# A graph attention layer with residual norm: f2 spread by one transpose, f1 made early, bounds moved among the table work, two tiles requested ahead

## The reference

```
in_fts = W @ x.T
f1 = (w1 @ in_fts).T + b1            # one number for each row
f2 = (w2 @ in_fts).T + b2            # one number for each column
logits = leaky_relu(f1 + f2.T)       # slope 0.01
coefs = softmax(logits + where(adj > 0, 0, -1e9), axis=-1)
out = layernorm(x + coefs @ x)       # over the 128 columns, eps 1e-5
```

## Time and profile before

| | us |
|---|---|
| median of 3 runs | 318.31 |
| lowest, highest | 314.53, 329.12 |
| the profiled execution | 315.71 |
| its span, first to last instruction | 313.9 |
| TensorE, matmuls busy | 266.3 |
| VectorE busy | 243.3 |
| ScalarE busy | 189.2 |
| GpSimd busy | 49.0 |

### The profile page before, as it was taken

The page is one execution under the profiler, slowest core; times in us unless marked ns, Lnnn a source line. Parts: engine busy times, 40 slices in busy tenths (PEclk is TensorE's granted clock), DMA queues, the critical chain, the costliest instruction groups (busy, mean ns, idle before and its releaser), DMA issues.

```text
span 313.9 us, 5895 instructions
## 1 busy us (share of the span) xinstructions
PE 266.3 (85%) x2178; PEld 225.0 (72%) x2178; DVE 243.3 (78%) x338; ACT 189.2 (60%) x270; POOL 49.0 (16%) x50
## 2 busy tenths in 40 slices
PE   1889580394999959996999999999999999999980
PEld 1745480273788848884888888888888888888860
DVE  1768794739575859996998999999699779899432
ACT  0619377619989195739857974987877792131130
POOL 3000013000000000350072027008101200331200
PEclk9999895599699999997999999999999999999997
DMA  4999949409999999999999999999999999510011
GB/s 128 309 326 244 204 106 216 82 2 226 309 310 305 303 304 301 304 304 275 303 310 289 325 333 325 291 319 320 290 291 318 322 276 269 139 36 1 0 45 25
DMA packets 25598, 73.64 MB, mean 235 GB/s; under 512 B 3440, under 2 KB 7664, under 8 KB 25584
## 3 DMA queue, kind: packets, MB, share of 16 engines
q1 hardware_dynamic: 14800, 36.77, 41.4%
q10 hardware_dynamic: 10144, 34.61, 38.1%
q0 software_dynamic: 640, 2.10, 3.2%
HBM read 71.37 MB, written 2.10 MB: 234 GB/s over the span
## 4 chain that ended last, share of the span: by engine, by line
PE 54%; ACT 12%; DVE 11%; DMA 10%; issue 6%; ACTq 3%; POOL 3%; POOLq 0%; DVEq 0%
PE ps L960 51%; ACT sgn L405 8%; DMA nat<-in_adj 7%; DMA msk<-in_x 2%; ACTq L271 2%; DVE msk L623 1%; POOL nmr L366 1%; PE ps L940 1%; ACT post L498 1%; DVE f2raw L557 1%; DVE sgn L553 1%; DVE bt L600 1%; ACT bt L437 1%; DVE mn L615 1%; DVE post L594 1%
## 5 line engine op out<-in xcount | busy, mean ns | idle before, releaser
L960 PE MATMUL ps<-bt,msk 128*128 128x258 f16 x2048 | 237.5, 278 | 14.3 <-ACT post L498 10.6
L960 PEld LDWEIGHTS ps<-bt,msk 128*128 128x128 fp8e5 x2048 | 203.3, 100 | 48.1 <-issue 11.4
L405 ACT ACTIVATE sgn<-ps,nf1l 128x1024 int8<-128x1024 f32 x128 | 132.1, 1137 | 19.8 <-DVE mn L615 11.1
L610 DVE TENSOR_SCALAR mn<-nat 128x4096 int8<-128x4096 int32 x32 | 72.6, 2283 | 27.2 <-DMA nat<-in_adj 26.3
L498 ACT ACTIVATE post<-ps,ac 128x258 f32<-128x258 f32 x64 | 27.8, 502 | 44.7 <-PE ps L960 44.7
L366 POOL TENSOR_SCALAR nmr<-mv 128x4 f32<-128x4 f32 x7 | 21.2, 3025 | 199.8 <-DVE mv L775 199.8
L623 DVE STREAM_TRANSPOSE msk<-mn 128x1024 uint32<-128x1024 uint32 x32 | 37.9, 1220 | 0.0
L615 DVE SCALAR_TENSOR_TENSOR mn<-sgn,mn 128x1024 uint32<-128x1024 uint32 x32 | 37.7, 1217 | 0.0
L505 ACT ACTIVATE ybt<-ybt,nmr,rstd 128x128 f32<-128x128 f32 x28 | 11.5, 484 | 17.0 <-POOL nmr L371 17.0
L628 DVE TENSOR_SCALAR msk<-msk 128x1024 uint32<-128x1024 uint32 x32 | 20.1, 666 | 0.0
L600 DVE SCALAR_TENSOR_TENSOR bt<-bt,post 128x1024 f16<-128x1024 f16 x8 | 9.8, 1219 | 6.7 <-ACT bt L437 6.7
(11 more groups left out here) (93 smaller groups left out, 109.4 us busy)
## 6 DMA issues: line engine op xcount, KB each, us to landing
nat<-in_adj SPq DMA_DIRECT2D x64, 512.0 KB, 18.9
nat<-in_adj ACTq DMA_DIRECT2D x64, 512.0 KB, 15.4
xn<-in_x POOLq DMA_DIRECT2D x4, 512.0 KB, 8.6
out<-ybt SPq DMA_DIRECT2D x28, 64.0 KB, 21.0
msk<-in_x SPq DMA_DIRECT2D x8, 128.0 KB, 6.0
msk<-in_x ACTq DMA_DIRECT2D x8, 128.0 KB, 7.0
out<-post SPq DMA_DIRECT2D x16, 16.0 KB, 1.5
wsb<-in_L_gnn_W SPq DMA_DIRECT2D x1, 64.0 KB, 2.3
```

What stands on the lines that cost most here:

```text
L405: ins = act.activation(sgn[:, c, g * JA:(g + 1) * JA], f2b, ACT.Sign, bias=nf1l[:, bass.ds(G * t + g, 1)], scale=-1.0)
L610: dve.tensor_scalar(mn[:, c % 2], nat[:, c], 0, EDGE, ALU.is_gt, ALU.mult).then_inc(cast_done, 1)
L960: ins = pe.matmul(ps[:, 2 * s + m, 0:2 * DV], mask_f[c][m][:, n // KB, n % KB, :], btv[m][:, n, :], start=(n == 0), stop=(n == NK - 1))
```

## The change

1. `f2b` is a tile in SBUF, written by one VectorE transpose of 32x32 blocks (`f2_rows`), whose input repeats each value of `f2l` 32 times. `spread_f2`, the four matmuls behind it and their PSUM banks go.
2. w1 and w2 are loaded as two rows (`wrow`), and TensorE turns them into `w12`. The first chunk of x is requested ahead of W, w1 and w2.
3. All of `turn_x`, `xT_out` and `f1_columns` run before the first edge sums, in two PSUM banks by turns; statistics go to bank 3. `signs` can take another piece of work between its second and third activation.
4. VectorE's list is ordered anew: `spread_f1(1)`, f1n, the statistics, the bounds, `ea` and `flag` stand between the steps of the tables, and the flag is no longer behind them all. TensorE sums xsum ahead of tile 0's m = 0 chunks; the fourth set of signs stands before the flag.
5. Tiles 4 and 5 are requested by both queues before the flag, each once the cast of tile 0 or 1 has freed its slot.

The diff, without declarations of semaphores and the general branch:

```diff
+        f2b = sb("f2b", [P, JA], F32)
+        wrow = sb("wrow", [2, P], F32)
...
-        f2b = ps[:, 4:6, :].rearrange("p b n -> p (b n)")
         FIRST = 3
-        turn_bank = [0, 1, 2, 0, 2, 3, 2, 3]
...
+            for a in range(A // 2):
+                load_x(sp, a, 0)
             sp.dma_start(wsb[:, :], W).then_inc(w_in, 16)
-            for h in range(BCH):
+            for h in range(1, BCH):
...
+            for c in range(EARLY):
+                load_tile(1, c)
             go = fast(sp)
...
+                load_quad(1, first=EARLY)
...
-            act.dma_start(w12[:, 0:1], w1.rearrange("o h -> h o")).then_inc(w12_in, 16)
-            act.dma_start(w12[:, 1:2], w2.rearrange("o h -> h o")).then_inc(w12_in, 16)
-            for h in range(BCH):
+            for a in range(A // 2, A):
+                load_x(act, a, 0)
+            act.dma_start(wrow[0:1, :], w1).then_inc(w12_in, 16)
+            act.dma_start(wrow[1:2, :], w2).then_inc(w12_in, 16)
+            for h in range(1, BCH):
...
-            def signs(t, c):
...
+                    ins = act.activation(sgn[:, c, g * JA:(g + 1) * JA], f2b[:, :], ACT.Sign,
                                          bias=nf1l[:, bass.ds(G * t + g, 1)], scale=-1.0)
+                    if g == 1 and between:
+                        between()
...
-                act.activation(xT[:, b * 512:(b + 1) * 512], ps[:, turn_bank[b], :], ACT.Copy).then_inc(xT_ready, 1)
+                act.activation(xT[:, b * 512:(b + 1) * 512], ps[:, 4 + b % 2, :], ACT.Copy).then_inc(xT_ready, 1)
...
             xT_out(1)
             f2_sums(4, 8)
             xT_out(2)
+            square(0)
+            xT_out(3)
             load_far(1, 1)
-            xT_out(3)
             act.wait_ge(f2l_ready, 1)
             act.activation(de[:, :], f2l[:, :], ACT.Exp, scale=NEG_SLOPE).then_inc(exp_ready, 1)
             scales(1, de)
+            xT_out(4)
             act.wait_ge(nF2_ready, 1)
             act.activation(be[:, :], f2l[:, :], ACT.Exp, bias=nF2[:, 0:1]).then_inc(exp_ready, 1)
             scales(0, be)
-            act.wait_ge(f2b_made, 1)
+            xT_out(5)
+            act.wait_ge(f2b_ready, 1)
             act.wait_ge(nf1l_ready, 1)
-            signs(0, 0)
+            signs(0, 0, between=lambda: xT_out(6))
             split_x(1, 0)
-            square(0)
+            xT_out(7)
             split_x(1, 1)
+            square(1)
+            square(2)
+            split_x(1, 2)
+            square(3)
             load_far(2, 2)
-            square(1)
-            xT_out(4)
-            split_x(1, 2)
-            xT_out(5)
             split_x(1, 3)
-            xT_out(6)
+            signs(1, 1, between=lambda: split_x(0, 0))
+            split_x(0, 1)
             load_far(3, 3)
-            split_x(0, 0)
-            xT_out(7)
-            square(2)
-            square(3)
-            signs(1, 1)
-            split_x(0, 1)
             split_x(0, 2)
-            split_x(0, 3)
-            signs(2, 2)
+            act.wait_ge(cast_done, 1)
+            load_far(QT, 0)
+            signs(2, 2, between=lambda: split_x(0, 3))
+            act.wait_ge(cast_done, 2)
+            load_far(QT + 1, 1)
+            act.wait_ge(nf1l_ready, 2)
+            signs(3, 3)
             act.wait_ge(ea_ready, 1)
             act.activation(ac[:, :, :], ea[:, :, :], ACT.Exp).then_inc(rows_ready, 1)
             act.wait_ge(rows_ready, 1)
...
-                ahead(0, 0, 4)
+                ahead(0, 0, 4, True)
                 evacuate(0, 0, 0)
-                ahead(0, 1, 4)
+                ahead(0, 1, 4, True)
                 evacuate(0, 0, 1)
...
-            def spread_f2(half):
-
-                n = NK // 2
-                dve.tensor_tensor(spread[:, half * 512:(half + 1) * 512].rearrange("p (b r k) -> p b r k", r=SQ, k=KB),
-                                  f2l[:, half * n:(half + 1) * n].rearrange("p (b o k) -> p b o k", o=1, k=KB
-                                                                            ).to_broadcast([P, NB // 2, SQ, KB]),
-                                  pick[:, None, :, None].to_broadcast([P, NB // 2, SQ, KB]),
-                                  ALU.mult).then_inc(spread_ready, 1)
+            def f2_rows():
+
+                dve.transpose(f2b.rearrange("p (b r k) -> p b k r", r=SQ, k=KB),
+                              f2l.rearrange("p (b k o) -> p b k o", k=KB, o=1).to_broadcast([P, NB, KB, SQ])
+                              ).then_inc(f2b_ready, 1)
...
+            dve.wait_ge(w12_made, 1)
+            dve.tensor_copy(w12[:, :], ps[:, 6, 256:258]).then_inc(w12_ready, 1)
             dve.wait_ge(v_made, 1)
...
-            spread_f2(0)
-            spread_f2(1)
+            f2_rows()
             stat_max(0, 0, 2)
...
             scale_x(1, 0)
-            scale_x(1, 1)
             cast(0, 0, 0)
             low_den(1)
+            scale_x(1, 1)
+            combine(0, 0)
             low_x(1, 0)
+            turn(0, 0)
             scale_x(1, 2)
-            combine(0, 0)
+            plus(0, 0)
             low_x(1, 1)
-            turn(0, 0)
-            dve.wait_ge(f2b_made, 1)
+            spread_f1(1, FIRST * KB, NK, 7, 0)
             scale_x(1, 3)
-            plus(0, 0)
             low_x(1, 2)
+            dve.wait_ge(nf1_made, 2)
+            for g in range(G):
+                rows = slice(g * SQ, (g + 1) * SQ)
+                dve.tensor_scalar(f1n[rows, :], ps[rows, 6, 128:256].rearrange("p (t g) -> p t g", g=G)[:, :, g], -1.0,
+                                  None, ALU.mult).then_inc(f1n_ready, 1)
+            dve.tensor_copy(nf1l[:, FIRST * KB:], ps[:, 6, 128 + FIRST * KB:256]).then_inc(nf1l_ready, 1)
             dve.wait_ge(cs_ready[0], 1)
             scale_x(0, 0)
             low_x(1, 3)
+            dve.wait_ge(f1n_ready, G)
+            dve.tensor_reduce(stat[:, 2:3], f1n[:, :], AX_X, ALU.max, apply_absolute_value=True)
+            dve.wait_ge(squares_ready, BCH)
+            dve.tensor_reduce(stat[:, 3:4], squares[:, :], AX_X, ALU.add).then_inc(stat_ready, 1)
             low_den(0)
             scale_x(0, 1)
+            stat_max(1, 2, 4)
             cast(1, 1, 0)
             low_x(0, 0)
+            stat_out(1, 2, 4)
             scale_x(0, 2)
-            low_x(0, 1)
-            combine(1, 1)
-            scale_x(0, 3)
-            turn(1, 1)
-            low_x(0, 2)
-            plus(1, 1)
-            low_x(0, 3)
-            spread_f1(1, FIRST * KB, NK, 7, 384)
-            dve.wait_ge(squares_ready, BCH)
-            dve.tensor_reduce(stat[:, 3:4], squares[:, :], AX_X, ALU.add)
-            dve.wait_ge(nf1_made, 2)
-            for g in range(G):
-                rows = slice(g * SQ, (g + 1) * SQ)
-                dve.tensor_scalar(f1n[rows, :], ps[rows, 7, 128:256].rearrange("p (t g) -> p t g", g=G)[:, :, g], -1.0,
-                                  None, ALU.mult).then_inc(f1n_ready, 1)
-            dve.tensor_copy(nf1l[:, FIRST * KB:], ps[:, 7, 128 + FIRST * KB:256]).then_inc(nf1l_ready, 1)
-            dve.wait_ge(f1n_ready, G)
-            dve.tensor_reduce(stat[:, 2:3], f1n[:, :], AX_X, ALU.max,
-                              apply_absolute_value=True).then_inc(stat_ready, 1)
-            stat_max(1, 2, 4)
-            stat_out(1, 2, 4)
-
             dve.tensor_tensor(rng[:, 0:1], gst[:, 0:1], gst[:, 1:2], ALU.add).then_inc(rng_step, 1)
             dve.scalar_tensor_tensor(out=rng[:, 1:2], in0=gst[:, 0:1], scalar=gst[:, 1:2], in1=gst[:, 2:3],
                                      op0=ALU.max, op1=ALU.add).then_inc(rng_step, 1)
+            low_x(0, 1)
             dve.wait_ge(rng_step, 2)
             dve.tensor_scalar(rng[:, 2:3], rng[:, 0:1], F2_SPAN, None, ALU.is_le).then_inc(rng_step, 1)
             dve.tensor_scalar(gsum[:, :], f1n[:, :], gst[:, 0:1], None, ALU.add).then_inc(row_step, 1)
+            combine(1, 1)
...
+            scale_x(0, 3)
             dve.wait_ge(rng_step, 4)
...
+            turn(1, 1)
             dve.wait_ge(rng_step, 5)
             dve.scalar_tensor_tensor(out=flag[:, :], in0=gst[:, 3:4], scalar=X_MIN ** 2 * NK * D, in1=rng[:, 0:1],
                                      op0=ALU.is_ge, op1=ALU.mult).then_inc(flag_ready, 1)
+            low_x(0, 2)
+            plus(1, 1)
+            low_x(0, 3)
             dve.wait_ge(xsum_made, 1)
-            dve.tensor_reduce(xsum[:, :], ps[:, 6, :].rearrange("p (k d) -> p d k", d=D), AX_X,
+            dve.tensor_reduce(xsum[:, :], ps[:, 4, :].rearrange("p (k d) -> p d k", d=D), AX_X,
...
-                pe.transpose(ps[0:c1 - c0, 7, (1 + j) * P:(2 + j) * P], stat[:, c0:c1],
+                pe.transpose(ps[0:c1 - c0, 3, (1 + j) * P:(2 + j) * P], stat[:, c0:c1],
...
-                if b in (3, 6, 7):
-
-                    pe.wait_ge(xT_ready, {3: 1, 6: 5, 7: 6}[b])
+                if b >= 2:
+                    pe.wait_ge(xT_ready, b - 1)
...
+            pe.wait_ge(consts_ready, 1)
             pe.wait_ge(w12_in, 32)
```

(56 more changed lines are left out.)

38 lines of the change are left out of this document (16 added, 22 removed).

## The result

The changed kernel takes 302.86 us (median of 4 runs, 302.23 to 307.30); the kernel before took 321.34 in the same comparison (4 runs). The ratio is 0.9565, interval 0.9424 to 0.9705. Some executions of a kernel take some per cent longer than its others; the ratios leave these out, and a kernel with fewer than three others has none. Two controls in later rounds, the changed kernel unaltered with more runs of the kernel before beside it, gave 0.9698 (0.9635 to 0.9761) and 0.9733 (0.9669 to 0.9797): some 3% is the better figure, 9 us. The profiled execution took 302.5 us, its span is 300.8, 13.1 less than before.

What follows compares the result with a forecast made beforehand. TensorE's start of tile 2 and its later stops were taken to bound the kernel; 11.8 + 1.5 + 5 = 18.3 us won took the span from 313.9 to 295.6, forecast time 298.5, range 293 to 308.

Steps and rivals of the forecast that it cites:

- rival A: Only the head's gain stays: crowded queues land tiles 6 and 7 late, or VectorE stalls at `split_x`; 303 to 308, chance 0.20.
- f2 by rows: VectorE's chain before tile 2: one 1.22 us transpose replaces two spreads, four matmuls leave TensorE; `scale_x(1, 0)` 2.6 us sooner.
- First `combine`: VectorE in `combine(0, 0)`: a new wait of 2.4 us for ScalarE's signs, bounds 2 and 3.5.
- Flag at 54: VectorE's flag, moved amid the table work, falls at about 54 us against 68.32.
- No wait for `split_x`: VectorE's four waits for ScalarE's `split_x` before the cast of tile 2, 6.7 us together, should go.
- The start of tile 2: TensorE's first matmul of tile 2 at 66.8 us in place of 78.62: 11.8 us won.
- The slow clock: TensorE idles about one us before tile 2, not 4.36, so 1.5 of 2.6 us lost to slow clock are won.
- the sum: Span as TensorE's start of tile 2, 1920 matmuls, stops, slow clock and tail: 313.8 before, changed term by term.
- The stops: TensorE's two later stops of 3.32 and 2.92 us: the first goes, the second goes or shrinks to 0.5; 5 of 6.2 won.
- The weights: Weights loaded as rows behind two loads of x on each ring: cost taken as 0, range -1 to +1.6 us.
- C: Rival: tile 3's far half queues behind other loads, in at 65 us at 203 GB/s; slower kernel below about 125; chance 0.04.
- B: Rival: TensorE bounds the head, xsum at half speed and cold matmuls end tile 1 at about 72; 309 or 306; chance 0.12.

Runs made afterwards that it cites:

- e2: Changed kernel with VectorE's wait for xn moved from ahead of `pair(1, 0, 1)` to behind `pair(3, 1, 1)`; 304.65 us, ratio to before 0.9689.
- e10: Changed kernel with weights requested ahead of x, VectorE's xn wait behind the casts of tiles 2 to 7, ScalarE's normalise later; 295.62 us, ratio to before 0.9390.
- e1: Changed kernel with the early requests of tiles 4 and 5 undone, requested behind the flag as before; 312.24 us, ratio to before 0.9961.
- e3: Changed kernel with VectorE's wait for xn later and xn also loaded only when four tiles are cast; 314.74 us, no ratio given.
- e7: Changed kernel with ScalarE's normalise moved behind the second evacuation of the quad after next; 299.92 us, ratio to before 0.9507.

## Why the prediction was right, and where it was off

The direction and the range held (293 to 308); the forecast of 298.5 was 4.4 us low, and the gain of 18.3 us came to 13.1 by the spans and to some 9, half of it, by the two controls. That the range held owes something to its width: the controls' 304.6 and 305.5 us lie where rival A put its share.

- f2 by rows: `gst` forecast at 20.8, was 20.85; `scale_x` 21.3, was 21.47. The transpose took 2.00 us, not 1.22, inside its bounds and with nothing behind it. Right.
- First `combine`: wait of 2.4 forecast (2 to 3.5), 3.22 measured. Flag at 54: 54.26. No wait for `split_x`, 0.8 for the statistics. Right; VectorE was free for the cast of tile 2 at 58.1 plus 0.9, against 58.4.
- The start of tile 2, "I take 66.8": 70.50. This is the step that failed. I had moved xn's load forward to 31 and counted its bytes, but not looked up who waits for it. It now shares the DMAs with the halves of tiles 2 to 5, took up to 26.7 us to land in place of 11, and VectorE's wait for it stands in front of tile 2. That wait spans 3.5 of the 3.7 us. But only some 1.5 of them are xn's alone: the far half of tile 3, in at 63.3 where 61 was reckoned, would have kept the other 2.0. In the three executions of this kernel the wait for xn, without the flag's 0.9, was 3.5, 4.1 and 1.0 us; e2, without it, began tile 2 at 69.26, still 2.5 behind the 66.8.
- The slow clock: 1.5 forecast, 0.1 came: the first 512 matmuls took 60.22 us, 2.6 above the later pace (57.6), nearly as before (2.75). The rule in the sum was that TensorE idles for one us before tile 2; it idled for 4.96, since the start was late, and the page shows the clock at 6 there again. In e2 and e10, with 1.47 of idling, no slice there is under 9. The 1.3 us that the matmuls gave in the sum above came later, most of it from the 1408 behind before's last stop (159.32 us, 0.9 above that pace).
- The stops: "I take 5 of the 6.2", 3.5 came. The first went, as forecast, since tiles 4 and 5 were there. The second, ahead of tile 10, shrank to 0.98, not to nothing, and in the controls it stayed at 2.05 and 2.76 of 2.92. New ones of 0.2 to 0.8 came. I take their cause to be the data's pace, which I had set aside with "a little faster than TensorE uses them up"; for these short stops it isn't shown. That remark read a mean over a stretch in which TensorE itself held the requests back. e1 and e3 show that there is no slack in it.
- The weights: I took 0 of a range up to 1.6. The changed kernel's own profile bears that out (f2l at 17.38 against 18.11 before), the controls do not: 1.3 to 1.5 later than before, near the late end of the range. Here the Trainium skill was nearer than my row: "DMA: Bandwidth & Descriptors", "Queues, rings and completion order", has descriptors taken in ring order, and the landings of W (5.6 to 8.0 us behind x, 1.8 to 1.9 in front of it) agree.
- Rival A named the right mechanism for what was missing, the crowded queues, but placed it at tiles 6 and 7; it struck first at xn and tile 3. The measured time lies where its range begins. Of C a part came: tile 3's far half landed at 63.3, near the 65 that C gives for 203 GB/s and 2 us late, but the longer wait for xn hid it, and the kernel wasn't slower. B did not: xsum took 9.2 us, over at 54.

So each number of the sum's head was within a us, up to one wait that was in plain view in the list of instructions and the landings behind it. The sum's form holds for reading a profile; as a forecast it fails where it takes the stops as fixed while the start moves (e1, e3).

What stays open: what share of e7's gain is the dips and what share the stops themselves, and what a kernel would gain whose queues each load parts for both halves of the partitions, so that a queue left alone would still write both.

## What to carry to other kernels

When a load is moved forward, look up every wait on its semaphore: it competes with new neighbours there, and a wait that cost nothing may stand in front of the path. When a long wait is lifted, look at what has landed behind it: here a second transfer was 2 us late and hidden. An earlier start and data ahead were each worth little alone in this kernel; check the term of the stops after each change, since they take up what was won in front of them. A DMA share near 1 does not say that the DMAs move what they can: read the GB/s beside it, which partitions the transfers under way write, and whether an engine that issues requests is waiting for something else.
